# Row statistics moved from VectorE to ScalarE, and weight slots of a feed-forward phase freed one by one

## The reference, cut to what matters

```python
x = x + 0.5 * ffn(layernorm(x), w_gate, w_up, w_down)
x = x + attn(layernorm(x), ...)
x = x + 0.5 * ffn(layernorm(x), w_gate, w_up, w_down)

def act_quant(x):                       # per row
    scale = 127.0 / clip(max(abs(x), axis=-1), 1e-5)
    return clip(round(x * scale), -128, 127) / scale
def bitlinear(x, w): return act_quant(x) @ weight_quant(w).T   # w: -1, 0 or 1, times one number
def ffn(x):          # x: rows x 1024, gate and up: 4096 x 1024, down: 1024 x 4096
    return bitlinear(silu(bitlinear(x, w_gate)) * bitlinear(x, w_up), w_down)
```

## Time and profile before

| | us |
|---|---|
| median of 2 runs | 12624.29 (12618.74 to 12629.84) |
| the profiled execution, slowest core | 12731.51 |
| its span on that core (core 4) | 12730.0 |
| spans of cores 0 to 3 in it | 12541.2 to 12572.8 |
| PE busy in the span | 7081.1 (56%) |
| DVE / ACT / POOL busy | 4464.2 (35%) / 2262.4 (18%) / 439.5 (3%) |
| DMA moved | 1498.99 MB, mean 118 GB/s |

### The profile page before, as it was taken

How to read it: one execution, slowest core, us unless ns; L and a number is a source line. 1 busy time by engine, 2 the same in 40 slices (tenths; PEclk the granted TensorE clock), 3 DMA queues, 4 the chain that set the end, 5 groups by cost and what they waited for, 6 DMA issues and landing times. The chain is left out here.

```text
span 12730.0 us, 91328 instructions; the slowest of 8 cores (12541.2 to 12730.0 us)
## 1 busy us (share of the span) xinstructions
PE 7081.1 (56%) x29647; PEld 3103.5 (24%) x30210; DVE 4464.2 (35%) x8346; ACT 2262.4 (18%) x2093; POOL 439.5 (3%) x646
## 2 busy tenths in 40 slices
PE   0000467667767776633333444445766777677767
PEld 0000123223323333221211111112332333233323
DVE  3331243344434434345451111113333333343333
ACT  1110122222322322200001111111112211221121
POOL 0000000000000000021210000000000000000000
PEclk9999988888888888855556777778888888888888
DMA  2333444444344444322323223223434433344333
GB/s 85 106 99 91 127 135 145 146 135 151 138 147 136 158 147 137 135 78 74 84 66 106 61 61 87 63 61 123 156 136 132 144 134 136 129 136 145 136 129 116
DMA packets 1143404, 1498.99 MB, mean 118 GB/s; under 512 B 1026520, under 2 KB 1026521, under 8 KB 1091996
## 3 DMA queue, kind: packets, MB, share of 16 engines
q1 hardware_dynamic: 72236, 1009.10, 20.4%
q10 hardware_dynamic: 1006912, 250.01, 10.8%
q0 software_dynamic: 63792, 234.00, 5.6%
HBM read 1076.71 MB, written 166.46 MB: 98 GB/s over the span
## 5 line engine op out<-in xcount | busy, mean ns | idle before, releaser
L552 PE MATMUL pp<-f_wb,f_q1T 128*128 128x512 bf16 x8028 | 3252.7, 405 | 2247.0 <-DMA f_wb<-wuT 846.7
L553 PE MATMUL pp<-f_wb,f_q1T 128*128 128x512 bf16 x8027 | 3245.4, 404 | 32.2 <-DVE f_t L508 16.1
L630 PE MATMUL pp<-f_wb,f_qT 128*128 128x512 bf16 x8030 | 1863.4, 394 | 599.3 <-DVE f_pr L558 589.2
L558 DVE SCALAR_TENSOR_TENSOR f_pr<-pp,f_au,f_sl 128x1024 bf16<-128x1024 f32 x512 | 657.6, 1284 | 3471.1 <-ACT f_sl L556 3471.1
L552 PEld LDWEIGHTS pp<-f_wb,f_q1T 128*128 128x128 bf16 x8192 | 844.2, 103 | 3405.5 <-issue 2638.8
L630 PEld LDWEIGHTS pp<-f_wb,f_qT 128*128 128x128 bf16 x8192 | 822.6, 101 | 1639.9 <-issue 812.4
L556 ACT ACTIVATE f_sl<-pp,f_ag 128x1024 bf16<-128x1024 f32 x512 | 570.0, 1113 | 3215.6 <-PE pp L553 2585.8
L553 PEld LDWEIGHTS pp<-f_wb,f_q1T 128*128 128x128 bf16 x8192 | 841.1, 103 | 1080.3 <-issue 305.4
L583 ACT ACTIVATE f_sv<-f_pr,p_mag,f_s 128x1024 f32<-128x1024 bf16 x512 | 634.9, 1240 | 1185.3 <-DVE f_s L575 726.5
L894 PE MATMUL pp<-a_w,a_pT 128*128 128x512 bf16 x1004 | 369.8, 545 | 759.3 <-DMA a_pT<-a_gg 756.4
L744 PE MATMUL pp<-c_Ur,c_tp 128*128 128x32 bf16 x2048 | 286.6, 215 | 568.7 <-DMA c_tp<-kpad 543.9
(11 more groups left out here) (169 smaller groups left out, 4491.5 us busy)
## 6 DMA issues: line engine op xcount, KB each, us to landing
f_wb<-wgT SPq DMA_DIRECT2D x128, 2048.0 KB, 14.0
f_wb<-wuT SPq DMA_DIRECT2D x128, 2048.0 KB, 18.9
f_wb<-wdT SPq DMA_DIRECT2D x64, 4096.0 KB, 12.6
c_tp<-kpad POOLq DMA_DIRECT2D x256, 256.0 KB, 4.0
f_x<-x SPq DMA_DIRECT2D x16, 2048.0 KB, 9.9
x1b<-f_x POOLq DMA_DIRECT2D x64, 512.0 KB, 4.0
a_x<-x1b SPq DMA_DIRECT2D x8, 4096.0 KB, 13.0
x2b<-a_x POOLq DMA_DIRECT2D x64, 512.0 KB, 2.9
```

Source lines behind the costliest of these rows:

```text
L552: mm1 = s.do("tensor", lambda e, l=lhs, rh=rhs_g, p=pg, h=half, j=j: e.matmul(p[:, h * 512:(h + 1) * 512], l, rh, start=(j == 0), stop=(j ...
L553: mmt = s.do("tensor", lambda e, l=lhs, rh=rhs_u, p=pu, h=half, j=j: e.matmul(p[:, h * 512:(h + 1) * 512], l, rh, start=(j == 0), stop=(j ...
L558: pv1 = s.do("vector", lambda e, p=pu, c0=c0, pc=pcol: e.scalar_tensor_tensor(out=s_pr[:, pc:pc + 1024], in0=p[:, :], scalar=st_au[:, c0:c ...
L630: last_mm = s.do("tensor", lambda e, q=r * 4 + ib, k=k, p=pd, h=half, i2=i2: e.matmul(p[:, h * 512:(h + 1) * 512], s_qTl[q][:, k * 128:(k ...
```

## The change

Four edits, all in `ffn_phase`:

1. buildA_rt: the row sum and the sum of squares are no longer VectorE reductions. ScalarE makes two passes over the tile, a Copy and a Square, and each gives its row sum through `accum_out`. Two reductions of 128x1024 leave VectorE, one pass comes to ScalarE, and the square no longer waits for VectorE's reduction of the tile before.
2. emit_ln: the same two sums in the same way.
3. `pending_ln` is called after groups 2, 5, 8 and 11, in place of groups 1, 3, 5 and 7.
4. buildC: slot 0 is free after the last tile's `i2` = 7 and slot 1 after its `i2` = 15, in place of the last matmul. Slots 2 and 3 stay as they were.

```diff
-                        a1 = s.do("vector", lambda e, xs=xs, c0=c0: e.reduce_sum(st_m1[:, c0:c0 + 1], xs, AX), [tx], "vv")
                         a2 = s.do("vector", lambda e, xs=xs, c0=c0: e.reduce_max(st_t1[:, c0:c0 + 1], xs, AX), [tx], "vv")
                         a3 = s.do("vector", lambda e, xs=xs, c0=c0: e.tensor_reduce(st_t2[:, c0:c0 + 1], xs, AX, ALU.min), [tx], "vv")
-                        sq = s.do("scalar", lambda e, xs=xs: e.activation(s_sq2[:, :], xs, AF.Square), [tx, sv_free], "sv")
-                        a4 = s.do("vector", lambda e: e.reduce_sum(st_sq[:, :], s_sq2[:, :], AX), [sq], "vv")
-                        sv_free = a4
+                        a1 = s.do("scalar", lambda e, xs=xs, c0=c0: e.activation(s_sq2[:, :], xs, AF.Copy, scale=1.0, accum_out=st_m1[:, c0:c0 + 1]), [tx, sq_last], "sv")
+                        sq = s.do("scalar", lambda e, xs=xs: e.activation(s_sq2[:, :], xs, AF.Square, accum_out=st_sq[:, :]), [tx, a1], "sv")
+                        sq_last = sq
...
-                            if oq <= 1 and pending_ln and r % 2 == 1:
+                            if pending_ln and (oq * RP2 + r) % 3 == 2:
                                 pending_ln.pop(0)()
...
-                    i1 = s.do("vector", lambda e, bo=bo, r=r, c0=c0: e.reduce_sum(st_t1[:, c0:c0 + 1], s_x[:, bo + r * 1024:bo + (r + 1) * 1024], AX), [h1], "vv")
-                    i2a = s.do("scalar", lambda e, bo=bo, r=r: e.activation(s_sq2[:, :], s_x[:, bo + r * 1024:bo + (r + 1) * 1024], AF.Square), [h1, sv_free], "sv")
-                    i3 = s.do("vector", lambda e, c0=c0: e.reduce_sum(st_t2[:, c0:c0 + 1], s_sq2[:, :], AX), [i2a], "vv")
-                    sv_free = i3
+                    i1 = s.do("scalar", lambda e, bo=bo, r=r, c0=c0: e.activation(s_sq2[:, :], s_x[:, bo + r * 1024:bo + (r + 1) * 1024], AF.Copy, scale=1.0, accum_out=st_t1[:, c0:c0 + 1]), [h1, sq_last], "sv")
+                    i3 = s.do("scalar", lambda e, bo=bo, r=r, c0=c0: e.activation(s_sq2[:, :], s_x[:, bo + r * 1024:bo + (r + 1) * 1024], AF.Square, accum_out=st_t2[:, c0:c0 + 1]), [h1, i1], "sv")
+                    sq_last = i3
...
+                                    if r == RP2 - 1 and i2 in (7, 15) and half == 1:
+                                        slot_last[i2 // 8] = last_mm
...
-                    for i_ in range(4):
-                        wslot_tok[i_] = last_mm
+                    wslot_tok[0] = slot_last[0]
+                    wslot_tok[1] = slot_last[1]
+                    wslot_tok[2] = last_mm
+                    wslot_tok[3] = last_mm
```

More of the change, by code:

```diff
@@ L466, in ffn_phase @@
                 u_free = None
-                sv_free = None
                 prev_svr = None
+                sq_last = None
                 state = {}
@@ L488, in buildA_rt @@
                     tx = st["tx"]
-                    nonlocal sv_free, prev_svr, u_free
+                    nonlocal prev_svr, u_free, sq_last
                     if True:
@@ L492, in buildA_rt @@
                         c0 = stc(m, r)
-                        a1 = s.do("vector", lambda e, xs=xs, c0=c0: e.reduce_sum(st_m1[:, c0:c0 + 1], xs, AX), [tx], "vv")
                         a2 = s.do("vector", lambda e, xs=xs, c0=c0: e.reduce_max(st_t1[:, c0:c0 + 1], xs, AX), [tx], "vv")
                         a3 = s.do("vector", lambda e, xs=xs, c0=c0: e.tensor_reduce(st_t2[:, c0:c0 + 1], xs, AX, ALU.min), [tx], "vv")
-                        sq = s.do("scalar", lambda e, xs=xs: e.activation(s_sq2[:, :], xs, AF.Square), [tx, sv_free], "sv")
-                        a4 = s.do("vector", lambda e: e.reduce_sum(st_sq[:, :], s_sq2[:, :], AX), [sq], "vv")
-                        sv_free = a4
+                        a1 = s.do("scalar", lambda e, xs=xs, c0=c0: e.activation(s_sq2[:, :], xs, AF.Copy, scale=1.0, accum_out=st_m1[:, c0:c0 + 1]), [tx, sq_last], "sv")
+                        sq = s.do("scalar", lambda e, xs=xs: e.activation(s_sq2[:, :], xs, AF.Square, accum_out=st_sq[:, :]), [tx, a1], "sv")
+                        sq_last = sq
                         b1 = s.do("vector", lambda e, c0=c0: e.tensor_scalar(out=st_m1[:, c0:c0 + 1], in0=st_m1[:, c0:c0 + 1], scalar1=1.0 / H, scalar2=None, op0=ALU.mult), [a1], "vv")
-                        b2 = s.do("vector", lambda e: e.tensor_scalar(out=st_sq[:, :], in0=st_sq[:, :], scalar1=1.0 / H, scalar2=None, op0=ALU.mult), [a4], "vv")
+                        b2 = s.do("vector", lambda e: e.tensor_scalar(out=st_sq[:, :], in0=st_sq[:, :], scalar1=1.0 / H, scalar2=None, op0=ALU.mult), [sq], "vv")
                         b3 = s.do("vector", lambda e, c0=c0: e.scalar_tensor_tensor(out=st_B[:, c0:c0 + 1], in0=st_m1[:, c0:c0 + 1], scalar=st_m1[:, c0:c0 + 1], in1=st_sq[:, :], op0=ALU.mult, op1=ALU.subtract), [b1, b2], "vv")
@@ L597, in emit_ln @@
                 def emit_ln(m, bo, r, c0, tidx, h1):
-                    nonlocal u_free, sv_free
-                    i1 = s.do("vector", lambda e, bo=bo, r=r, c0=c0: e.reduce_sum(st_t1[:, c0:c0 + 1], s_x[:, bo + r * 1024:bo + (r + 1) * 1024], AX), [h1], "vv")
-                    i2a = s.do("scalar", lambda e, bo=bo, r=r: e.activation(s_sq2[:, :], s_x[:, bo + r * 1024:bo + (r + 1) * 1024], AF.Square), [h1, sv_free], "sv")
-                    i3 = s.do("vector", lambda e, c0=c0: e.reduce_sum(st_t2[:, c0:c0 + 1], s_sq2[:, :], AX), [i2a], "vv")
-                    sv_free = i3
+                    nonlocal u_free, sq_last
+                    i1 = s.do("scalar", lambda e, bo=bo, r=r, c0=c0: e.activation(s_sq2[:, :], s_x[:, bo + r * 1024:bo + (r + 1) * 1024], AF.Copy, scale=1.0, accum_out=st_t1[:, c0:c0 + 1]), [h1, sq_last], "sv")
+                    i3 = s.do("scalar", lambda e, bo=bo, r=r, c0=c0: e.activation(s_sq2[:, :], s_x[:, bo + r * 1024:bo + (r + 1) * 1024], AF.Square, accum_out=st_t2[:, c0:c0 + 1]), [h1, i1], "sv")
+                    sq_last = i3
                     i4 = s.do("vector", lambda e, c0=c0: e.tensor_scalar(out=st_t1[:, c0:c0 + 1], in0=st_t1[:, c0:c0 + 1], scalar1=1.0 / H, scalar2=None, op0=ALU.mult), [i1], "vv")
@@ L613, in buildC @@
                 def buildC(m, twd1, twd2, post_r=None):
-                    nonlocal u_free, sv_free
+                    nonlocal u_free
                     st = state[m]
@@ L618, in buildC @@
                     last_mm = None
+                    slot_last = [None, None]
                     for r in range(RP2):
```

## The result

| | before | after |
|---|---|---|
| median of the runs of the same chip job, us | 12,658.62 (10 runs, 12,583.06 to 12,767.41) | 13,279.17 (11 runs, 13,207.33 to 13,377.09) |
| ratio, 95% interval | | 1.0496 (1.0457 to 1.0535) |
| the profiled execution, us | 12,731.51 | 13,260.05 |
| its span, us | 12,730.0 (core 4) | 13,258.5 (core 7) |

The change makes the kernel 5.0% slower, by 621 us between the medians. The forecast was 12,830 with a range up to 12,930. The direction was right and the size was not.

A forecast was written before the change was run, and what follows sets the result against it. A block's length was taken as TensorE's matmuls plus its stalls. Terms of +195 (group 12), +20 (borders) and -6 us (small things) gave +209 on the median of 12,624.3, so 12,830 us, range 12,580 to 12,930.

The forecast's parts named there:

- emit_ln behind group 11 and the x load ahead of the weights: Ahead of group 12, first phase: weights issued 8.0 us later plus 5.9 us of x load bytes, 14 x 13.9 = +195 us.
- rival of a cheap x load: Ahead of group 12: the x load's bytes take nothing from the weight loads, 112 us in all, time 12,750; chance 0.13.
- accum_out as a plain pass: ScalarE's sums in the preparation and emit_ln: a pass with accum_out costs the plain pass's 1.06 us, the lower end taken.
- dear sums: Rival on ScalarE: accum_out passes cost twice the plain pass, 64 us at borders and 30 in emit_ln, 12,924; chance 0.12.
- The border: Between blocks: idle time moves from ahead of group 0 to group 1, which starts 0.6 us later; +20 us over 30 borders.
- All 8 MB end 10.3 us earlier, less some 1.0 us: Weight loads at the border: the transposition that landed at 2930.2 lands at 2920.9; with 3 us lost, +2.6 us a border.
- first rival: At the border, tile 1's transposition slips through between the load pairs; group 1 9.4 us earlier, 12,532 us; chance 0.16.
- 1 to 2 us of hole are needed at every border: Argument against tile 1's transposition slipping through: the two pairs of weight loads would need such a gap each time.
- the 18 us: Time tile 2's transposing DMA took among the weight loads before, against a median of 3.1; read as showing queues give no protection.
- The relief of VectorE: Some 2.4 us of reductions a tile taken off VectorE, said to be worth nothing elsewhere since VectorE waits there.

The follow-up runs named there:

- e1: The changed kernel with all four weight slots freed by the last matmul again, as before the change; 12,841.66 us, 1.0194 of the kernel before.
- e3: The changed kernel with only the sums moved to ScalarE, slots and emit_ln places as before the change; 12,599.36 us, 0.9997 of the kernel before.
- e8: The changed kernel with the x load issued behind the first half of wdT and slice 3's weights; 13,122.97 us, 3.3% above the kernel before.
- e4: The kernel before with only the early freeing of slots 0 and 1 added; 12,971.44 us, 1.0280 of the kernel before.
- e6: The changed kernel with the stores of tiles 1 and 2 issued behind tile 3's; 12,849.64 us, 1.0101 of the kernel before.
- e9: The kernel before with slice 3's gate and up loads issued right behind slice 2's, ahead of the x load and twd1; 11,924.42 us, 0.9337 of the kernel before.

## Why the prediction was wrong

- **emit_ln behind group 11 and the x load ahead of the weights: right.** +195 us forecast; 209 by the count, 203 by the idle time between e1 and e3, and 240 by the medians of e1 and before. The lateness was 8.18 us for 8.0, and the rest of the 14.9, some 6.7 us, agrees with the 5.9 of the x load's bytes; e8 shows that SP's order is the way it acts, and moves both at once. The rival of a cheap x load is out: it gave 8.0 us a block, and 14.9 were lost.
- **accum_out as a plain pass: right**, 1.06 us plus a read of 0.19. The dear sums are out. The group of the Square with its sum in after, whole span:

```profile
L496 ACT ACTIVATE f_sq<-f_x 128x1024 f32<-128x1024 f32 x128 | 135.2, 1057 | 12.0 <-ACT f_sq L495 0.4
```

- **The border: the failed step.** It is the end of the weight loads, the step that said "All 8 MB end 10.3 us earlier, less some 1.0 us", with 3 us as the upper end "if two streams disturb each other". The path was right: group 0 early (6.6 us for 14.6), the wait at tile 2 and no longer at tile 3, the whole preparation of tile 3 behind it, group 1 released by L633. But the loads did not end 9.3 us earlier. In before the last one landed 24.1 us behind buildC (mean of the 80 borders for which the trace has the landing); in after it was 16.2 us at the borders that slip through and 19.6 at the caught ones, and 35.5 at the long ones, 11 us later than before. The transposition of tile 1 landed at 31.3 us there, where the step had it at 18.5, and the preparation of tile 3 and group 1 came behind it: group 1 was 16.7 us later than before at 139 of 240 borders. +20 us was said with +78 as its bound; +303 is what the count gives as a mean of all cores. The medians, which are of the slowest core, give more: 3.0 points of the ratio (1.0496 less e1's 1.0194), some 380 us. The mean over the cores of e4's runs gives 298 us for this edit alone, the slowest cores 350.
- **The range.** The bound of 3 us came from no row. I had read steady states only, loads of one queue issued together (357 GB/s ahead of group 12, and the four loads of the border), and carried them over to an arrangement of three queues that no trace showed: two staggered pairs, a transposition and a store. Such a term has no upper bound from rows of a steady state, and the range should have said so.
- **The first rival happens**, at 25 borders of 240, and mostly once the store is out of the way (e6: 183). The rival's arithmetic gives group 1 at 19.4 us; it stands at 20.3 at those 183 and at 21.7 at the 25, so its price was nearly right. Against it I had put that "1 to 2 us of hole are needed at every border". Read with the 18 us as proof, this was too strong. In the Trainium skill, "DMA: Bandwidth & Descriptors", section "Queues, rings and completion order", the engines serve the queues in turn; e6 agrees so far that a transposition issued at 12,112.90 no longer held L517 at 12,122.59, while at the caught borders it ends with the loads.
- **The relief of VectorE is worth nothing: right** (e3, 0.9997).

## What to carry to other kernels

Freeing a buffer earlier moves a transfer, and what counts is what it then runs beside: here 10 us of earlier loads cost 10 us of later work. Ask first who waits for the small transfer in the middle of the large one. In an issuing queue that works in order, look for a load whose buffer has been free for long and that stands behind one whose buffer hasn't: two lines of order (e9) were worth 6.6%, more than anything else that was tried. And work taken off an engine that is waiting for a transfer only lengthens its wait.

## What the runs showed of the hardware

- With three queues of DMA in one stretch (16 KB rows of weights in two pairs, a transposition and a 512 KB store) a core's transfer rate fell far at 139 of 240 borders, in the one shown to 169 GB/s at 0.66 busy for 34 us, against 308 to 378 GB/s at 0.95 or more in the other border windows shown. The last 1.0 MB of it took 20 us. It is not the same at every border of one program: 76 caught and 25 free ones stand beside the long ones.
- A sum through `accum_out` costs ScalarE 0.19 us on a pass of 128x1024.
- TensorE's mean granted clock (1 is full speed) fell from 0.809 on before's slowest core to 0.796 on after's; in the windows above it is 0.63 in the long border and 0.99 in the one that slips through.
